# Moving weight sums and low halves to GpSimd, low halves of gated products to VectorE, and product copies ahead of high halves

## What is computed

```
x   = x + softmax(norm(scores(layernorm(x), ctx)))      # cross attention
xn  = layernorm(x)
w   = router(xn)                                        # a weight per token and expert, 8 experts
gate_e = xn @ Wg[e] (+ xn @ Ga[e] @ Gb[e] for e < 2)
up_e   = xn @ Wu[e] (+ xn @ Ua[e] @ Ub[e] for e < 2)
mid_e  = silu(gate_e) * up_e
out_e  = mid_e @ Wd[e] (+ mid_e @ Da[e] @ Db[e] for e < 2)
x   = x + sum_e w[:, e] * out_e
```

## Time and profile before

| | |
|---|---|
| median of 3 runs | 1147.43 us (1147.41 to 1148.15) |
| the profiled execution | 1149.48 us |
| its span, first to last instruction | 1147.8 us |
| mean granted clock of PE | 0.981 of full |
| busy: DVE, ACT, POOL | 68%, 38%, 23% of the span |

### The profile page before, as it was taken

How to read it: one execution, slowest core, us unless ns; L and a number is a source line. 1 busy time by engine, 2 the same in 40 slices (tenths; PEclk the granted TensorE clock), 3 DMA queues, 4 the chain that set the end, 5 groups by cost and what they waited for, 6 DMA issues and landing times.

```text
span 1147.8 us, 12310 instructions
## 1 busy us (share of the span) xinstructions
PE 1070.2 (93%) x4680; PEld 862.9 (75%) x4680; DVE 776.0 (68%) x1155; ACT 440.6 (38%) x634; POOL 259.8 (23%) x184
## 2 busy tenths in 40 slices
PE   6899999688999999999999969899999999999998
PEld 4787777466887878787877758677777878787777
DVE  6788795849486675749485692866757484857743
ACT  3454242343344344434343333443433342534430
POOL 2511144204030221304030210402213040403122
PEclk8899999889999999999999979999999999999999
DMA  8310002253132331414150205102111111211111
GB/s 295 120 46 1 1 15 84 57 176 128 37 116 68 97 105 56 147 55 129 37 181 22 73 18 202 56 19 74 37 56 55 55 38 37 73 36 57 37 38 74
DMA packets 85692, 86.35 MB, mean 75 GB/s; under 512 B 4096, under 2 KB 61568, under 8 KB 84864
## 3 DMA queue, kind: packets, MB, share of 16 engines
q1 hardware_dynamic: 85344, 85.49, 22.9%
q10 hardware_dynamic: 288, 0.07, 0.0%
HBM read 70.86 MB, written 14.68 MB: 75 GB/s over the span
## 4 chain that ended last, share of the span: by engine, by line
PE 55%; DVE 25%; issue 10%; ACT 6%; DMA 3%; SPq 0%; POOL 0%; DVEq 0%; ACTq 0%; POOLq 0%
PE tiles L1361 9%; PE tiles L1363 9%; PE tiles L1362 9%; PE gate_up L1471 6%; PE gate_up L1473 6%; PE gate_up L1472 6%; DVE mids L1131 5%; DVE wd_lo L1093 3%; ACT piece_hi L725 3%; DVE piece_lo L1085 2%; DVE piece L1073 2%; DVE piece L1074 2%; PE gate_up L1430 1%; PE gate_up L1429 1%; PE gate_up L1435 1%
## 5 line engine op out<-in xcount | busy, mean ns | idle before, releaser
L527 POOL TENSOR_TENSOR mids_lo<-mids,mids_hi 128x512 fp32r<-128x512 f32 x112 | 181.5, 1638 | 555.2 <-ACT mids_hi L759 554.6
L1471 PE MATMUL gate_up<-xT_hi,piece_hi 128*128 128x512 f32 x448 | 179.1, 400 | 29.8 <-ACT u_sb L745 28.1
L1085 DVE TENSOR_TENSOR piece_lo<-piece,piece_hi 128x1024 fp32r<-128x1024 f32 x112 | 133.7, 1235 | 106.0 <-ACT piece_hi L725 106.0
L1137 DVE SCALAR_TENSOR_TENSOR xacc<-tiles,rw,xacc 128x512 f32<-128x512 f32 x112 | 78.0, 750 | 163.0 <-PE tiles L1363 163.0
L1361 PE MATMUL tiles<-wd_hi,mids_hi 128*128 128x512 f32 x448 | 176.4, 394 | 9.6 <-POOL mids_lo L527 5.8
L1362 PE MATMUL tiles<-wd_lo,mids_hi 128*128 128x512 f32 x448 | 176.0, 393 | 0.0
L1363 PE MATMUL tiles<-wd_hi,mids_lo 128*128 128x512 f32 x448 | 175.9, 393 | 0.0
L1472 PE MATMUL gate_up<-xT_hi,piece_lo 128*128 128x512 f32 x448 | 175.9, 393 | 0.0
L1473 PE MATMUL gate_up<-xT_lo,piece_hi 128*128 128x512 f32 x448 | 175.4, 391 | 0.0
L1471 PE MATMUL gate_up<-tx_hi,piece_hi 128*128 128x512 f32 x336 | 133.9, 398 | 19.9 <-ACT s_sb L735 16.4
L1472 PE MATMUL gate_up<-tx_hi,piece_lo 128*128 128x512 f32 x336 | 132.3, 394 | 0.0
(11 more groups left out here) (165 smaller groups left out, 1559.6 us busy)
## 6 DMA issues: line engine op xcount, KB each, us to landing
piece<-in_wg_dram SPq DMA_DIRECT2D x40, 256.0 KB, 3.2
piece<-in_wu_dram SPq DMA_DIRECT2D x40, 256.0 KB, 3.3
wd_raw<-in_wd_dram SPq DMA_DIRECT2D x10, 1024.0 KB, 5.1
piece<-merged SPq DMA_DIRECT2D x32, 256.0 KB, 3.3
merged<-lora_w SPq DMA_DIRECT2D x6, 1024.0 KB, 5.3
w_raw<-in_xT_dram SPq DMA_DIRECT2D x4, 1024.0 KB, 6.1
wd_raw<-merged SPq DMA_DIRECT2D x4, 1024.0 KB, 5.6
out_dram<-xacc SPq DMA_DIRECT2D x16, 256.0 KB, 4.5
```

What stands on the lines that cost most here:

```text
L527: nc.gpsimd.tensor_tensor(mids_lo[h][:, f, :], mids[h][:, f, :], plain(mids_hi[h][:, f, :]), ALU.subtract)\
L1085: ins = nc.vector.tensor_tensor(piece_lo[j % 3][:, first:last, :], piece[j % 3][:, first:last, :], plain(piece_hi[j % 3][:, first - 1:last ...
L1137: nc.vector.scalar_tensor_tensor(tile_of(b, t), tiles[:, t, :], rw[:, (b * TT + t) * E + s:(b * TT + t) * E + s + 1], tile_of(b, t), ALU.m ...
L1471: nc.tensor.matmul(dst, w_h, x_h, start=first and kt == 0, stop=False, skip_group_check=True)
```

## The change

- **ACT order**: in a usual step `copy_p1`, `copy_p5` and `copy_u2` of the first quarter stand in front of `piece_high_part(j + 1)` and of the high half of C21; the three copies of quarter 4k+3 stand together, behind the high halves of C12, C11 and C22 as before, and ahead of that of C21; `piece_high_part(j + 4)` now stands behind `copy_u2(j + 2)`, and right before `wd_high_part`.
- **POOL**: makes the sums and low halves of nearly all pieces, and the low halves of Wd. In each usual step its order is: sums and low halves of pieces j+1, j+2, j+3, j+4, then low halves of Wd. (DVE keeps pieces 0, 1 and 29.)
- **DVE**: makes the low halves of the gated products and of the low-rank factor b instead.
- **Token sums**: at the start DVE makes them, between the units of block 3. `x_spill` keeps high and low halves (4 MB in place of 2 MB). At the seam three operands come back by DMAs that POOL issues straight into their place (`load_again`), and the sums are made by DVE during step 6, from what SP loads in five further steps (`load_back`), with one of them stored and loaded once more (`x21_spill`).
- SP issues `load_next_piece(3)` before it waits for the stored accumulator.

The new POOL program, and the orders around the up quarters (cut):

```diff
+            for f in range(FT):
+                low_part(B - 1, f)
+            pool.wait_ge(x_stored, 64)
             for k in range(STEPS):
-                if k < len(LORA_JOBS):
-                    lora_b_low_part(k)
-                for m in range(2):
-                    for c in (C12, C11, C22, C21):
-                        mid_low_part(k, m, c)
+                j = 4 * k
+                if k == SWAP:
+                    load_again(0, 0, 1)
+                    load_again(1, 2, 3)
+                    load_again(0, 2, 2)
+                if k not in (0, SWAP):
+                    piece_sums(j + 1)
+                    piece_low_part(j + 1)
+                piece_sums(j + 2)
+                piece_low_part(j + 2)
+                if k in (0, SWAP):
+                    wd_low_part(k)
+                piece_sums(j + 3)
+                piece_low_part(j + 3)
+                piece_sums(j + 4)
+                piece_low_part(j + 4)
+                if k not in (0, SWAP):
+                    wd_low_part(k)
```

ACT, usual step (after the change, from its start):

```diff
+                    mid_high_part(k - 1, 1, C12)
+                    copy_p1(j)
+                    mid_high_part(k - 1, 1, C11)
+                    copy_p5(j)
+                    mid_high_part(k - 1, 1, C22)
+                    copy_u2(j)
+                    mid_high_part(k - 1, 1, C21)
+                    piece_high_part(j + 1)
...
                     copy_p1(j + 2)
                     copy_p5(j + 2)
+                    copy_u2(j + 2)
                     piece_high_part(j + 4)
-                    copy_u2(j + 2)
-                wd_high_part(k)
+                    wd_high_part(k)
                 for c in (C12, C11, C22):
                     mid_high_part(k, 0, c)
                 copy_p1(j + 3)
                 copy_p5(j + 3)
+                copy_u2(j + 3)
+                mid_high_part(k, 0, C21)
                 if k in (0, SWAP):
                     piece_high_part(j + 4)
-                mid_high_part(k, 0, C21)
-                copy_u2(j + 3)
```

DVE, up quarters and start of the next step:

```diff
                 combine(k, UP, 0, C12)
...
                 combine(k, UP, 0, C11)
                 make_mid(k, 0, C12)
                 combine(k, UP, 0, C22)
                 make_mid(k, 0, C11)
+                mid_low_part(k, 0, C12)
                 make_mid(k, 0, C22)
-                if k < len(LORA_JOBS):
-                    add_lora(k)
-                wd_low_part(k)
+                mid_low_part(k, 0, C11)
...
+                    mid_low_part(k, 0, C22)
+                    if lora:
+                        add_lora(k)
+                    make_mid(k, 0, C21)
                 combine(k, UP, 1, C12)
+                mid_low_part(k, 0, C21)
                 combine(k, UP, 1, C11)
                 make_mid(k, 1, C12)
...
                     combine(k - 1, UP, 1, C22)
                     make_mid(k - 1, 1, C11)
+                    mid_low_part(k - 1, 1, C12)
                     make_mid(k - 1, 1, C22)
+                    mid_low_part(k - 1, 1, C11)
```

DVE at the end of block 3 (the sums of step 0), and the seam in step 7:

```diff
+            dve.wait_ge(sim_mm, B * TT)
+            x_sum(0, 1, 0)
+            x_sum(1, 0, 0)
+            difference(tx_sum[:, 1, :], tx_sum[:, 0, :], tx_sum[:, 1, :])
             unit(B - 1, 0)
             read_logitsT(B - 1, tiles)
+            x_sum(2, 1, 2)
+            difference(t3_sum[:, :], tx_sum[:, 2, :], tx_sum[:, 0, :])
             unit(B - 1, 1)
...
+            x_sum(0, 0, 2)
             router(B - 1)
...
+                if k == SWAP:
+                    difference(x_back[:, 2, :], x_back[:, 2, :], x_back[:, 3, :])
+                    mid_low_part(k - 1, 1, C22)
+                    make_mid(k - 1, 1, C21)
+                    t_low_part(5, ...)
+                    t_low_part(6, ...)
+                    mid_low_part(k - 1, 1, C21)
+                    t_low_part(7, ...)
                     piece_sums(j + 1)
+                    t_low_part(8, ...)
                     piece_low_part(j + 1)
                     add_down(k - 1, 0)
                     add_down(k - 1, 1)
```

More of the change, by code:

```diff
@@ L518, in x_sum, with load_again @@
[L518 to L528, removed]
+            def load_again(b, first, product):
+                pool.wait_ge(p_mm[product], 4 * SWAP)
+                cols = slice((b * KT + first) * S, (b * KT + first + 2) * S)
+                for part, xT_part in enumerate((xT_hi, xT_lo)):
+                    pool.dma_start(xT_part[:, cols], x_spill[b, part, :, first * S:(first + 2) * S].bitcast(f32r)).then_inc(x_again[product], 16)
@@ new lines, in piece_low_part, with wd_low_part @@
+            def piece_low_part(j):
+                if j >= 4 * STEPS:
+                    return
+                pool.wait_ge(piece_hi_made, j + 1)
+                for first, last in ((1, 5), (5, 8)):
+                    ins = nc.gpsimd.tensor_tensor(piece_lo[j % 3][:, first:last, :], piece[j % 3][:, first:last, :],
+                                                  plain(piece_hi[j % 3][:, first - 1:last - 1, :]), ALU.subtract)
+                ins.then_inc(piece_ready[j % 3], 1)
+            def wd_low_part(k):
+                pool.wait_ge(wd_hi_made, k + 1)
+                for h in range(2):
+                    part = slice(2 * h, 2 * h + 2)
+                    ins = nc.gpsimd.tensor_tensor(wd_lo[:, part, :], wd_raw[:, part, :], plain(wd_hi[:, part, :]),
+                                                  ALU.subtract)
+                ins.then_inc(wd_ready, 1)
@@ L782, in _ @@
[L782 to L788, removed]
@@ L803, in _ @@
[L803 to L810, removed]
+                    act.wait_ge(p_mm[6], j)
+                    t_high_part(tx_hi[:, 2, :], x_back[:, 3, :], 7)
+                    mid_high_part(k - 1, 1, C21)
+                    act.wait_ge(p_mm[7], j)
+                    t_high_part(xT_hi[:, KT * S:KT * S + 2 * S], x_back[:, 0, :], 6)
@@ L811, in _ @@
+                    act.wait_ge(p_mm[4], j)
+                    t_high_part(tx_hi[:, 0, :], x_back[:, 2, :], 8)
+                    piece_high_part(j + 1)
+                if k in (0, SWAP):
+                    copy_p1(j)
+                    copy_p5(j)
+                    copy_u2(j)
+                    for c in (C12, C11, C22):
+                        gate_silu(k, 0, c)
+                    copy_p1(j + 1)
+                    piece_high_part(j + 2)
                     copy_p5(j + 1)
@@ L1304, in _ @@
-                if k != SWAP:
-                    piece_sums(j + 2)
-                    piece_low_part(j + 2)
-                if k not in (0, SWAP):
+                if k in (0, SWAP):
+                    for c in (C12, C11, C22):
+                        combine(k, GATE, 0, c)
+                    combine(k, GATE, 1, C12)
+                    combine(k, GATE, 1, C11)
+                    combine(k, GATE, 1, C22)
+                    if lora:
+                        lora_a_low_part(k)
+                        lora_b_low_part(k)
+                    combine(k, UP, 0, C12)
+                else:
+                    combine(k, GATE, 0, C12)
+                    mid_low_part(k - 1, 1, C21)
+                    combine(k, GATE, 0, C11)
+                    combine(k, GATE, 0, C22)
+                    if k == SWAP - 1:
+                        back_sum(0, 1, 4)
+                        back_sum(2, 3, 4)
```

341 lines of the change are left out of this document (175 added, 166 removed).

## The result

| | before | after |
|---|---|---|
| median | 1147.42 us (1147.35 to 1148.15) | 1180.56 us (1179.5 to 1181.41) |
| ratio, 95% interval | | 1.0287 (1.0269 to 1.0305): slower by 33.1 us |
| the profiled execution, its span | 1149.48, 1147.8 us | 1180.54, 1178.8 us |
| mean granted clock of PE | 0.981 | 0.961 |

A forecast was written before the change was run, and what follows sets the result against it. PE, 93% busy, was taken to bound the kernel, plus the gaps in which it stands. Steps +62.6, start -16.4 and seam -4.4 summed to +42, carried to the median: 1147.4 + 42 = 1189 us, range 1157 to 1210.

The forecast's parts named there:

- T: Start of a step's last quarter, 4k+3; the prediction timed POOL's, DVE's and ACT's operations from it.
- Usual step: Step without a low-rank job: product 6 waits 6.8 us for copy_p1, so 69.4 us against 63.6, +5.8.
- 2.4 us for the clock: Price of PE's lower clock after a wait above some 3.5 us, added to each such wait.
- Low-rank step: Step with 8 more matmuls: wait of 5.0 us plus restart and clock, 69.4 us against 63.8, +5.6.
- Start: Start of the second part: losses of 25.7 us before fall to 9.3, -16.4.
- 0.5 "for the rest": Allowance of 0.5 us for remaining losses at the start, within the 9.3 us left there.
- Seam: Around step 7: losses of 20.5 us before become 16.1, from down half 1 and pieces 31 and 32, -4.4.
- The first (no block, 1092): Rival: wide POOL operations don't block DVE, so copy_p1 is in time and nearly all step gaps go; 1092 us, chance 0.18.
- the second (the clock kept, 1159): Rival: the 6.8 us waits come in the steps, but PE's clock doesn't drop; 1159 us, chance 0.10.
- the third (longer seam): Rival: extra waits at the seam from SP's loads and DVE's back sums, 5 to 15 us more; 1195 to 1204, chance 0.10.
- 11 x 1.4 + 8: Upper margin of the range: 1.4 us each for wait and clock, 11 times, and 8 for start and seam.
- Waits up to 3.1 us don't pay it: Claim that PE waits up to 3.1 us don't incur the lower clock, priced at 2.4 us.

The follow-up runs named there:

- Experiments 1 and 2: halves512 and halves256, in that order: the changed kernel with POOL's low halves of pieces and Wd in narrower operations; 1122.78 and 1111.13 us.
- experiment 5: The changed kernel with the low halves of Wd moved back from POOL to DVE, behind the low half of C11; 1111.45 us, ratio to before 0.9686.
- experiment 3: The changed kernel with copy_p1 and copy_p5 of quarter 4k+3 ahead of the high half of C22 on ACT; 1134.84 us, ratio to before 0.9888.
- halves512: The changed kernel with POOL's low halves of pieces and Wd in operations of at most 512 columns; 1122.78 us, ratio to before 0.9776.
- halves256: The changed kernel with POOL's low halves of pieces and Wd in operations of 256 columns; 1111.13 us, ratio to before 0.9686.
- mixed_early_cast: The changed kernel with 256-column POOL operations in usual steps, wide ones in steps 0 and 7, where the piece is cast before copy_u2(4k+3); 1094.51 us.
- experiment 4: The kernel before with only copy_u2 of a usual step's first quarter ahead of the high halves of the piece and C21; 1146.43 us, ratio 0.9988.
- the last kernel: mixed_early_cast with copy_p1 of quarter 4k+3 also ahead of the high half of C22; 1088.33 us, ratio to before 0.9482.
- experiment 6: The kernel before with POOL's low halves of gated products in two operations of 256 columns instead of one of 512; 1130.15 us, ratio 0.9857.

## Why the prediction was right, and where its sizes were off

**The mechanism and its place: right.** The forecast had POOL start at T-1.6 and `copy_p1` start at T+10.3; they started at T-1.6 (863.50) and T+9.7 (874.80). The turns stand as written: product C12, product C11, low half C12 and product C22 were to end at T+1.4, 3.8, 6.8 and 9.8, and ended at T+1.3, 3.6, 6.4 and 9.1. Experiments 1 and 2 show that it is the length of POOL's instructions, experiment 5 that Wd's stand in the way, and experiment 3 that the place of the copy counts. The rule of the Trainium skill (SBUF — State Buffer, "Who interferes with whom"), that the two block each other for a whole instruction, is borne out by the halves512 and halves256 runs: 6.08, 1.75 and 0.83 us for the same bytes.

**Usual step: +5.8 forecast, +4.5 measured** (68.07 against 63.58 in step 9). Two terms of the sum were too large. The wait of 6.8 was 6.08: I gave each of DVE's three turns between POOL's operations 0.6 us, but POOL's four took 10.2 us instead of the 10.8 so reckoned. And 2.4 us for the clock, from stretches of 14 and 9 matmuls, was too much: 68.07 - 59.84 - 6.08 = 2.15 for restart and clock together, where I had 2.7. The half clock lasted 8 or 9 matmuls here. **Low-rank step: +5.6 forecast, +4.4 measured** (68.2 against 63.8 in the mean of steps 2 to 5), for the same reasons (4.30 instead of 5.0). Over ten steps that would be 12 us; the table's two rows show 8. Steps 2 to 5 and 9 to 12 make up 9.5, but steps 1 and 8 came to +5.6 each where +4.8 and +5.0 were forecast: the half clock that follows the waits ending at 259 and 744 lies in them.

**Start: -16.4 forecast, -14.7 measured**, and part of the loss that follows lies in step 1 (70.76 us, 2.6 above its neighbours; in the kernel before it was 1.3 above them). The first piece's low halves on DVE, 2.97 us late, were in the 0.5 "for the rest", and the low-rank product was forgotten as a place where POOL blocks DVE. Timeline of the kernel after:

```profile
237.67 4.59 POOL L566 TENSOR_TENSOR piece_lo<-piece,piece_hi 128x1024 fp32r<-128x1024 f32 x2 [1.81 <-ACT piece_hi L772]
...
239.28 1.31 DVE L1099 TENSOR_TENSOR lora_a_split<-lora_a,lora_a_split 64x512 fp32r<-64x512 f32 x1 [8.74 <-ACT lora_b_hi L708]
240.63 2.18 DVE L1210 TENSOR_TENSOR lora_b_lo<-lora_b,lora_b_hi 128x512 fp32r<-128x512 f32 x1
...
242.91 0.47 PE L1536 MATMUL tiles<-lora_b_hi,lora_a_split 128*128 128x512 f32 x1 [3.64 <-issue]
```

The row names no releaser ("issue"), but its operand `lora_b_lo` ends at 242.81, behind two of POOL's operations. The block isn't all of it: ACT's casts of the factors ended only at 239.25, as PE fell idle, and the two operations alone take some 1.4 us (0.69 each in the later steps), so about 2.1 of the 3.64 are POOL's doing. In halves256, with short operations, the wait was still 3.02. It stands in front of piece 3's and hides the 1.6 forecast for that. Piece 4 was forecast 4.2 late, and was 4.50.

**Seam.** Down half 1 was to wait 5 and waited 4.74; piece 31 3.5 and 3.04; piece 32 3.1 and 3.38. Steps 6 and 7 together came to -2.7 in place of +2.4, 5.1 better. Of that step 6 (6.08 and a shorter half clock) makes 1.1, piece 31, which kept its clock, 1.7, down half 1 about 1, and 1.5 is that the kernel before lost more there than I had counted (144.47 less 119.8 of matmuls is 24.7, against 20.5 and 2.7). `load_again` cost nothing that shows. Step 13's wait was 2.90 (forecast 2.8), but with the clock lost, which I hadn't given it.

**The rivals.** The first (no block, 1092) fell by the rows of T; the second (the clock kept, 1159) by the window 875.40 to 879.00 below; the third (longer seam) by the seam's own waits. The first one's 1092 is close to the 1094.5 of mixed_early_cast, nearly without the block, but partly by luck: usual steps took 61.0 there and not 59.9, and steps 6 and 7 gained 10.8 where the rival had 4.

**Its sum.** +42 was reckoned on the span, and 31.0 came: 11 too many. Against the medians the change is 33.1, since the profiled execution of before happened to be 2.0 above its median, so the forecast of the median is only 8.4 too high; those 2 us are luck. The range doesn't quite follow from its own terms: 11 x 1.4 + 8 gives 1212 at the top and 11 x 1.9 + 8 gives 1160 at the bottom.

## What to carry to other kernels

When work moves to GpSimd, ask first how long one of its instructions is and which VectorE operations with two SBUF inputs fall into it, and only then how busy it gets. Split what runs beside such a chain into short operations, though they cost more in all, and leave wide what the consumer itself waits for. A copy that PE waits for doesn't belong behind a result that such an operation makes, and a reordering that takes one wait away must be followed to the next one: in experiment 4 a wait of 1.36 us took the place of the 1.40 that went.

## What had not been expected of the hardware

**The clock isn't set by the length of the wait alone.** Windows of the kernel after, each from the end of a wait (2.97, 3.64, 4.30, 3.04, 3.38, 6.08 and 2.90 us; columns as above, the clock third from the end):

```profile
210.20:213.00 2.80, 2.79 (x7) 2.24 (x8) 1.30 (x4) 1.43 (x1) 0.00 (x0) 0.53 0.00 0
242.90:246.00 3.10, 3.09 (x14) 2.58 (x15) 3.10 (x6) 0.75 (x2) 3.02 (x4) 1.00 0.00 0
322.60:326.00 3.40, 3.37 (x9) 2.65 (x10) 3.40 (x4) 1.06 (x2) 2.63 (x4) 0.56 0.00 0
731.00:734.00 3.00, 2.96 (x13) 2.46 (x14) 3.00 (x4) 0.76 (x2) 3.00 (x3) 1.00 0.00 0
744.20:748.00 3.80, 3.73 (x9) 2.95 (x10) 2.85 (x3) 0.76 (x2) 3.72 (x5) 0.50 0.00 0
875.40:879.00 3.60, 3.57 (x8) 2.82 (x9) 1.70 (x2) 1.07 (x3) 2.42 (x3) 0.50 0.00 0
1145.00:1149.00 4.00, 3.92 (x10) 3.16 (x11) 0.86 (x2) 1.63 (x4) 0.00 (x0) 0.58 0.00 0
```

Waits of 3.64 and 3.04 kept 2.4 GHz, those of 2.97, 3.38 and 2.90 lost it, and behind some the clock fell only after the first matmuls (0.56 and 0.58). The same wait of 3.64 in front of the low-rank product, which kept it here, lost it in the last kernel:

```profile
244.40:246.00 1.60, 1.60 (x4) 1.31 (x5) 1.60 (x3) 0.00 (x0) 1.60 (x3) 0.50 0.00 0
```

The prediction's "Waits up to 3.1 us don't pay it" holds for the kernel before (3.13 kept the clock at 736.15) and was wrong for this one. What decides between 2.9 and 3.7 us wasn't tried and stays open.

**The first narrowing brings most.** From 1024 to 512 columns DVE's product fell by 436 ns in the mean, from 512 to 256 by 53 more, while POOL's cost for 1024 columns rose from 2.4 to 2.8 and 3.4 us. Each turn of DVE lengthens POOL's work, so the narrow operations look dearer in the trace than they are alone: the eight of Wd at the seam of halves256, with no such operation of DVE beside them, took 5.61 us, against 4.77 for the two wide ones at the same place. In the kernel before the same holds: with POOL's operations halved in experiment 6, DVE's product fell from 1049 to 888 ns.
